# Last row added to one coefficient of two spectra on POOL, in place of an addition to the four output tiles (autocorrelation attention and feed-forward, one core)

## What is computed

```python
q = layernorm(x)
corr = ifft(fft(q) * conj(fft(c))).real          # along the 512 positions
w, idx = top_k(corr, 12); w = softmax(w)
out = sum(w[i] * c[minimum(idx[i] + pos, 511)])   # a shift past the end gives the last row
x1 = x + out
y = x1 + h @ W.T + bias + low_rank_update(h)      # h = layernorm(x1), 2048 x 2048
```

## Time and profile before

| | us |
|---|---|
| median of 3 runs | 3066.55 |
| lowest, highest run | 3057.17, 3071.3 |
| the profiled execution | 3070.83 |
| its span in the trace | 3069.1 |
| PE busy in the span | 2793.4 |
| POOL busy | 2226.3 |
| DVE busy | 1845.0 |
| ACT busy | 1016.9 |
| mean granted TensorE clock | 0.959 of full |

### The profile page before, as it was taken

The page is one execution under the profiler, slowest core; times in us unless marked ns, Lnnn a source line. Parts: engine busy times, 40 slices in busy tenths (PEclk is TensorE's granted clock), DMA queues, the critical chain, the costliest instruction groups (busy, mean ns, idle before and its releaser), DMA issues. The chain is left out here.

```text
span 3069.1 us, 35980 instructions
## 1 busy us (share of the span) xinstructions
PE 2793.4 (91%) x12576; PEld 1653.4 (54%) x12576; DVE 1845.0 (60%) x4326; ACT 1016.9 (33%) x1809; POOL 2226.3 (73%) x1494
## 2 busy tenths in 40 slices
PE   5878766599999999999999999999999999999998
PEld 3545444356556655566556655565556655554444
DVE  5666567666776667756676666666665567652200
ACT  3655543433324333333333323333232232211100
POOL 5776768777887788878887788777887778744222
PEclk8989887799999999999999999999999999999999
DMA  7467667574657455565657456655656365637853
GB/s 280 135 184 204 174 194 165 123 237 144 227 201 215 163 190 201 196 203 181 220 189 223 162 184 219 193 177 198 218 177 179 133 232 184 185 130 251 271 197 112
DMA packets 444373, 586.90 MB, mean 191 GB/s; under 512 B 216864, under 2 KB 343072, under 8 KB 426528
## 3 DMA queue, kind: packets, MB, share of 16 engines
q1 hardware_dynamic: 444192, 584.60, 59.8%
HBM read 383.19 MB, written 151.00 MB: 174 GB/s over the span
## 5 line engine op out<-in xcount | busy, mean ns | idle before, releaser
L771 PE MATMUL f_ps<-f_whi,f_hhi 128*128 128x512 f16 x2048 | 783.0, 382 | 9.9 <-DVE f_y L1154 9.1
L773 PE MATMUL f_ps<-f_wlo,f_hhi 128*128 128x512 f16 x2048 | 781.6, 382 | 0.0
L775 PE MATMUL f_ps<-f_whi,f_hlo 128*128 128x512 f16 x2048 | 780.7, 381 | 0.0
L855 ACT ACTIVATE a_side<-a_ps 128x256 f32<-128x256 f32 (+1 forms) x192 | 87.4, 455 | 898.7 <-PE a_ps L736 729.2
L775 PEld LDWEIGHTS f_ps<-f_whi,f_hlo 128*128 128x128 f16 x2048 | 201.6, 98 | 245.9 <-issue 7.6
L773 PEld LDWEIGHTS f_ps<-f_wlo,f_hhi 128*128 128x128 f16 x2048 | 201.9, 99 | 240.8 <-issue 9.2
L657 PE MATMUL a_ps<-a_tv,fold 128*128 128x256 f32 x512 | 167.0, 483 | 173.7 <-ACT a_vk L855 173.7
L771 PEld LDWEIGHTS f_ps<-f_whi,f_hhi 128*128 128x128 f16 x2048 | 202.3, 99 | 223.3 <-issue 17.1
L713 PE MATMUL a_ps<-a_wt,lag_neg 128*128 128x256 f32 x1024 | 295.6, 412 | 0.0
L1027 POOL TENSOR_TENSOR a_zv<-a_zv,a_tw 128x512 f32<-128x512 f32 x128 | 159.9, 1271 | 185.5 <-DVE a_tf L1154 185.5
L1027 POOL TENSOR_TENSOR a_zu<-a_zu,a_tu 128x512 f32<-128x512 f32 x128 | 159.9, 1271 | 165.4 <-DVE a_tu L1154 165.4
(11 more groups left out here) (132 smaller groups left out, 5741.4 us busy)
## 6 DMA issues: line engine op xcount, KB each, us to landing
f_whi<-whi_scratch SPq DMA_DIRECT2D x128, 512.0 KB, 6.1
f_wlo<-wlo_scratch SPq DMA_DIRECT2D x128, 512.0 KB, 6.9
a_rows<-in_x_dram SPq DMA_DIRECT2D x62, 1024.0 KB, 6.5
vs<-in_ctx_dram SPq DMA_DIRECT2D x64, 512.0 KB, 6.0
xs<-in_x_dram SPq DMA_DIRECT2D x64, 512.0 KB, 7.4
parts_scratch<-a_so SPq DMA_DIRECT2D x64, 512.0 KB, 3.3
x_scratch<-a_rows SPq DMA_DIRECT2D x32, 1024.0 KB, 4.8
f_x1p<-x_scratch SPq DMA_DIRECT2D x32, 1024.0 KB, 5.1
```

Of the source, the lines that this page charges most:

```text
L771: nc.tensor.matmul(f_ps[:, t, :], h_hi[q][:, kq, rows_t], w_hi[u % WR][:, :, kq, :], start=(k == 0), stop=False)
L773: nc.tensor.matmul(f_ps[:, t, :], h_hi[q][:, kq, rows_t], w_lo[u % WR][:, :, kq, :], start=False, stop=False)
L775: mm = nc.tensor.matmul(f_ps[:, t, :], h_lo[q][:, kq, rows_t], w_hi[u % WR][:, :, kq, :], start=False, stop=(k == DB - 1))
L855: return nc.scalar.activation(out, source, ACT.Copy, **how)
```

## The change

`raise_output`, an addition over 128 partitions x 1024 elements on POOL, is gone. In its place ACT multiplies partition 0 of the last row by L = 512 right after it has made `twice`, in place, and POOL adds that row (1 partition x 256 elements) to coefficient zero of the two output spectra: once in `add_upper`, to zu, and once in `add_lower`, to zf. The inverse matrices for the output turn it into a constant over all positions. The stores now wait for `out_moved` (DVE's `part_output`), and `load_v` for `z_added`.

```diff
@@ load_v, store_parts (SP)
-                at_least(sp, out_raised, n - LB + 1)
+                at_least(sp, z_added, n - LB + 1)
...
-                sp.wait_ge(out_raised, n + 1)
+                sp.wait_ge(out_moved, n + 1)
@@ double_last (ACT)
                 copy(twice[:, :], last[n % LB][:, :], scale=2.0).then_inc(doubled, 1)
+                act.wait_ge(doubled, n + 1)
+                copy(last[n % LB][0:1, :], last[n % LB][0:1, :], scale=float(L)).then_inc(last_raised, 1)
@@ add_upper (POOL)
-                add(zu[:, 0:2, :], tu[:, 0:2, :], ALU.add)
+                add(zu[:, 0:2, :], tu[:, 0:2, :], ALU.add).then_inc(zu_added, 1)
                 add(zu[:, 2:4, :], tu[:, 2:4, :], ALU.subtract)
+                pool.wait_ge(zu_added, n + 1)
+                pool.wait_ge(last_raised, n + 1)
+                add(zu[0:1, 0, :], last[n % LB][0:1, :], ALU.add).then_inc(zu_raised, 1)
@@ add_lower (POOL)
-                add(zf[:, 0:2, :], tf[:, 0:2, :], ALU.add)
+                add(zf[:, 0:2, :], tf[:, 0:2, :], ALU.add).then_inc(zf_added, 1)
                 add(zf[:, 2:4, :], tf[:, 2:4, :], ALU.subtract)
+                pool.wait_ge(zf_added, n + 1)
+                add(zf[0:1, 0, :], last[n % LB][0:1, :], ALU.add)
                 pool.wait_ge(z_paired, n + 1)
+                pool.wait_ge(zu_raised, n + 1)
                 add(zu[:, 0:2, :], zv[:, 0:2, :], ALU.add)
                 add(zu[:, 2:4, :], zv[:, 2:4, :], ALU.add).then_inc(z_added, 1)
-
-            def raise_output(n):
-
-                pool.wait_ge(out_moved, n + 1)
-                add(so[:, :, :], last[n % LB][:, :].unsqueeze(1).broadcast_to([T, TB, CH]), ALU.add
-                    ).then_inc(out_raised, 1)
@@ the loop of POOL
-                if 1 <= w <= N:
-                    raise_output(w - 1)
```

More of the change, by code:

```diff
@@ L342, in flow @@
         out_moved = sem("a_out_moved")
-        out_raised = sem("a_out_raised")
+        last_raised = sem("a_last_raised")
+        zu_added = sem("a_zu_added")
+        zu_raised = sem("a_zu_raised")
+        zf_added = sem("a_zf_added")
         parts_out = sem("a_parts_out")
```

## The result

The changed kernel takes 3217.05 us (3213.88 to 3221.33), against 3065.71 us for the kernel before on the same chips: a ratio of 1.050 (1.047 to 1.0525). It is 151 us slower, in the direction of the forecast of 3083 us but far outside its range. Helper lines have moved: POOL's `add` is L1032 now (L1027 before), `largest` ends at L1219 (L1216), the two transforms of the values are at L660 (L657).

The account below looks back on a forecast made before the run. PE was taken to bound most passes, so only passes where PE stalls could move. Losses of 27.6 us less gains of 10.9 gave +16.7 us, a forecast median of 3083 us, range 3058 to 3106.

Parts of the forecast that it names:

- the term for a_minus_max: DVE's two-column negation: waits about 0.65 us longer in passes 10 to 12 and six first row passes, 5.9 us lost.
- passes without rows still at 40.2 us: Sign to look for: passes without residual rows, where PE never waits, keep their 40.2 us.
- Rival 3: a_minus_max misses gaps more often, also in passes without rows, at 1.25 us a miss: 3095 to 3120 us; chance 0.20.
- rival 2: a_minus_max waits for one POOL instruction only, so 7.2 and 2.4 us come back: about 3074 us; chance 0.15.
- The one-partition addition: On POOL in add_upper and add_lower: 0.73 us each, 0.67 not overlapped; lost 4.7 + 2.7 + 8.0 + 0.7 us.
- the 12 passes like 34: Row passes where add_upper's addition delays a_rows and the already waiting f_bn: 12 x 0.67 = 8.0 us lost.
- Rival 1: A one-partition addition costs next to nothing, so the kernel is not slower: 3048 to 3064 us; chance 0.10.
- ACT's copy: Copy of the last row before row_normalise and move_upper, delaying PE at the output: 16 x 0.35 = 5.6 us lost.
- The gain: Large POOL addition removed, stores earlier: 8.5 us in six first row passes, 2.4 us at the end, 10.9 in all.
- The last stall: PE's stall at the end, behind the last chunk's store, f_attn, row and f_y: from 5.39 to 3.0 us.
- the sum without a_minus_max: One-partition additions 16.1 us plus ACT's copy 5.6 less gains of 10.9: 10.8 us slower.

Follow-up runs that it names:

- The rounds with 128-partition instructions: Negation measured alone, rest of the computation left out: DVE asks at 110 moments beside six POOL additions of 128x512; 128x2 takes at most 1.30 us.
- full-height kernel: Changed kernel with both last-row additions over 128 partitions (128x256), ACT's copy multiplying the other partitions by zero: 3114.56 us.

## Why the prediction was wrong

- **The step that failed** is the term for a_minus_max: 5.9 us for nine row passes and nothing for the passes without rows ("passes without rows still at 40.2 us"). They took +121.6 us of the 151, and the wait there went from 0.45 to 4.8 us. I had shifted a_minus_max by 0.67 us in the row passes only, and let it miss one end at most. Rival 3 named the right mechanism and the right passes, but priced a miss at 1.25 us and gave 3095 to 3120 us; three ends are missed in a pass without rows. And I wrote that the cover there can't be read off a row. It could: a_vk done at 1001.90, PE's `upper` at 1003.01, 1.1 us. Against it a wait of 4.8 in place of 0.45 us leaves 3.2 us of stall; 3.13 were measured. The shape of the added instruction, which I had only priced for POOL, decides how long DVE waits; no row of the kernel before could show that, since none has a POOL addition over one partition. Why it does so stays open.
- **The warning that I read and dropped.** The earlier trace rows showed a DVE missing an end, and the earlier trace rows a wait of 3.12 us (behind a 4 us p_lo in pass 9). I took the first as a size, not as a sign that the wait may pass several ends. By the rule of the Trainium skill (SBUF — State Buffer, Who interferes with whom), which has the engine that comes first hold the shared pair for its whole instruction, the wait would be one instruction long. The rounds with 128-partition instructions agree, at most 1.30 us; the 1.60 us of the earlier trace rows do not, and behind a 1x256 instruction the trace shows up to 6.82 us. The measurement decides.
- **a_minus_max in the row passes**: it went to 1.01 us in passes 10 to 12 (predicted 1.0), but 2.50 us in first and third row passes. In the second and fourth it fell to 1.04 us, as rival 2 has it, and these 12 passes became 9.7 us shorter.
- **The one-partition addition**: 0.72 us (predicted 0.73). Both together cost 19.0 us by the medians (predicted 16.1). By the profiled executions it is 20.7: passes 2 to 8 4.0 (4.7), 9 to 12 2.8 (2.7), the 12 passes like 34 11.7 (8.0), the end 2.2 (0.7), third row passes nothing. DVE's wait for a_rows there is 1.20 us, where 1.2 was given. Rival 1, an addition for next to nothing, is out.
- **ACT's copy**: 8.9 us (predicted 5.6). It takes 0.416 us, and PE's wait at the output goes from 0.23 to 0.67 us (0.6 was given), 21 times where I had counted 16.
- **The gain**: 13.4 us (predicted 10.9). POOL's waits for f_attn in passes 17 to 57 are gone, the six first row passes give 12.4 us (8.5), the end 2.2 (2.4). The last stall itself did not go to 3.0 us; in the changed kernel the longest there is 7.4 us, of two that sum to 10.0 us against 9.1 before.

In the changed kernel, DVE's wait for a_rows between 657 and 2895 us as in the earlier trace rows, and then the timeline of pass 34 as in the earlier trace rows and of PE at the output in pass 35 as in the earlier trace rows:

```profile
DVE f_bn L1273 <- POOL a_rows L1032: 14.3, 12, 1.2
```

```profile
1577.58 2.47 DVE L1273 BATCH_NORM_STATS2 f_bn<-a_rows 128x6 f32<-128x512 f32 x4 [1.20 <-POOL a_rows L1032]
...
1585.79 1.04 DVE L1219 TENSOR_SCALAR a_minus_max<-a_top_a 128x2 f32<-128x2 f32 x1
...
1638.74 0.67 PE L754 MATMUL a_ps<-a_zu,outm 128*128 128x256 f32 x2 [0.67 <-issue]
```

So what the prediction worked out from rows (the sum without a_minus_max: 10.8 us, measured 14.5) stood in the main, though two of its three terms are off by 3 us and partly cancel, and one two-column instruction outweighed it more than nine times (151.3 less 14.5 us).

## What to carry to other kernels

A DVE instruction whose duration varies between rows of the same shape, as a_minus_max from 0.17 to 3.12 us, may be waiting for POOL inside its own bar, where no view of idle time shows it: before POOL's order is touched, list every such row beside POOL's, work out the slack behind it, and price it for the worst wait up to POOL's next stop, not for one instruction. Where a tiny instruction sits on such a chain, write it in the form that does not wait (here two 128x1 in place of one 128x2: 1.2% of the whole kernel, in the kernel before as well). A short POOL instruction over one partition is not cheap because it is short; its cost has to be looked for on DVE.

## What the runs showed of the hardware that I had not expected

- Measured by itself: behind a POOL tensor_tensor of 1x256, a 128x2 float32 tensor_scalar of DVE is passed over at every end until POOL has to wait for a semaphore, 82 of 82 asks, up to 6.82 us. Behind 1x512, 64x512, 128x256 and 128x2 it is not (at most 1.34 us). In the whole kernel 1x192 and 1x128 act like 1x256 (4.6 and 4.5 us in the passes without rows, one run each). Why this shape is not known.
- A semaphore wait that costs POOL 0.12 us (2.60 in place of 2.48 us for the two zu additions) lets DVE in; in the changed kernel it is worth 141 us.
- One partition saves POOL nothing: 1x256 takes 0.71 us and 128x256 0.72 us.
- A DVE tensor_scalar of 128x1 does not wait for POOL at all (0.153 to 0.155 us in 110 rounds).
- Not settled: in the row passes DVE is passed over at some ends without any 1x256 instruction before (2.27 us in the full-height kernel, 1.60 us in the earlier trace rows), and let in at others behind one, where POOL does not stop (1.04 us in pass 34, and so in all 12 second and fourth row passes and in 10 to 12 of the changed kernel). The measurement of the wait by itself showed neither.
